# Third layer of a four-layer AdaLN/FFN kernel: conditioning by 32x32 products, a two-strip router, and the share added by accumulating transfers

## What is computed

```python
def _L2_cond_ref(x, embedding, W0, b0, W1, b1, W2, b2, weight, bias_k):
    h = jax.nn.gelu(embedding @ W0 + b0, approximate=False)
    h = jax.nn.gelu(h @ W1 + b1, approximate=False)
    att = jax.nn.softmax((h @ W2 + b2) / T, axis=-1)      # 64 x 8
    agg_w = jnp.einsum('bk,koi->boi', att, weight[..., 0]) # a 32x32 matrix for each sample
    agg_b = att @ bias_k
    return jnp.einsum('boi,bih->boh', agg_w, x) + agg_b[:, :, None]

def _L2_ffn_ref(hidden_states, router_weight, router_bias, expert_bias):
    flat = hidden_states.reshape(T, H)                     # 2048 x 512
    logits = jnp.einsum('th,eh->te', flat, router_weight) + router_bias   # 64 experts
    scores = jax.nn.softmax(logits, axis=-1)
    topk_w, topk_idx = jax.lax.top_k(scores, 8)
    w_sum = topk_w.sum(axis=-1, keepdims=True)
    w_dense = jnp.zeros((T, E)).at[jnp.arange(T)[:, None], topk_idx].add(topk_w)
    bias_mix = jnp.einsum('te,eh->th', w_dense, expert_bias)
    return flat * w_sum + bias_mix
```

## Time and profile before

| | us |
|---|---|
| median of 3 runs | 560.16 |
| lowest, highest | 559.52, 560.53 |
| the profiled execution | 559.38 |
| its span | 557.6 |

### The profile page before, as it was taken

One profiled execution on the slowest core, in us unless ns is written; L12 is line 12 of the kernel. 1 busy time (PEld: TensorE's weight loads), 2 busy tenths in 40 slices (PEclk: granted clock), 3 DMA queues, 4 the chain that ended last, 5 costly groups with the idle time before them and its releaser, 6 DMA issues.

```text
span 557.6 us, 7199 instructions
## 1 busy us (share of the span) xinstructions
PE 543.6 (97%) x2689; PEld 418.3 (75%) x2689; DVE 256.3 (46%) x529; ACT 129.9 (23%) x227; POOL 192.5 (35%) x176
## 2 busy tenths in 40 slices
PE   7999999999999999999999999999999999989996
PEld 5788888888888888888888876353535799867784
DVE  3542343622225422126223327173442388897775
ACT  4322222322223222223222221000020022244332
POOL 2699990400001200002105700300002044589996
PEclk9999999999999999999999999999999999999999
DMA  9498230293000400000313007897920333120413
GB/s 311 151 421 308 76 97 0 75 155 89 0 0 0 132 37 0 0 0 1 94 41 94 1 0 100 146 142 213 164 84 12 94 96 94 19 38 2 150 59 113
DMA packets 84212, 50.33 MB, mean 90 GB/s; under 512 B 69600, under 2 KB 74464, under 8 KB 83424
## 3 DMA queue, kind: packets, MB, share of 16 engines
q1 hardware_dynamic: 82096, 38.97, 31.8%
q0 software_dynamic: 2016, 11.01, 5.5%
q10 hardware_dynamic: 80, 0.08, 0.0%
HBM read 31.93 MB, written 8.62 MB: 73 GB/s over the span
## 4 chain that ended last, share of the span: by engine, by line
PE 92%; DVE 5%; issue 1%; ACT 1%; DMA 1%; POOL 0%; DVEq 0%; POOLq 0%
PE ps L547 91%; DVE c_lo L963 1%; DVE cT L963 1%; DMA pack_a<-in_pack_a 1%; DVE t L963 0%; DVE rest L1145 0%; PE ps L693 0%; PE ps L731 0%; PE ps L787 0%; PE ps L737 0%; DVE wcat L963 0%; DVE c_lo_odd L963 0%; DVE m L1141 0%; DVE lg L963 0%; DVE rest L963 0%
## 5 line engine op out<-in xcount | busy, mean ns | idle before, releaser
L547 PE MATMUL ps<-c_lo,wl 128*128 128x512 f32 x448 | 173.0, 390 | 0.3 <-POOL c_lo L422 0.3
L547 PE MATMUL ps<-c_hi,wl 128*128 128x512 f32 x448 | 173.1, 390 | 0.2
L963 DVE TENSOR_TENSOR hff<-silu,ps 128x512 f32<-128x512 f32 x56 | 38.5, 687 | 160.3 <-PE ps L547 160.2
L547 PEld LDWEIGHTS ps<-c_lo,wl 128*128 128x128 f32 x448 | 84.1, 188 | 18.6 <-POOL c_lo L422 0.7
L547 PEld LDWEIGHTS ps<-c_hi,wl 128*128 128x128 f32 x448 | 84.1, 188 | 18.2 <-ACT c_hi L849 0.8
L547 PE MATMUL ps<-wl,h_hi 128*128 128x512 f32 x224 | 87.7, 391 | 0.0
L547 PE MATMUL ps<-wl,h_lo 128*128 128x512 f32 x224 | 87.2, 389 | 0.0
L963 DVE TENSOR_TENSOR h_lo<-hff,h_hi 128x512 fp32r<-128x512 f32 x56 | 49.0, 875 | 39.1 <-ACT h_hi L849 39.1
L422 POOL TENSOR_TENSOR c_lo<-cT,c_hi 128x512 fp32r<-128x512 f32 x8 | 10.7, 1341 | 156.9 <-ACT c_hi L849 156.9
L849 ACT ACTIVATE h_hi<-hff 128x512 fp32r<-128x512 f32 x56 | 35.4, 632 | 112.5 <-DVE hff L963 112.5
L883 ACT ACTIVATE silu<-ps 128x512 f32<-128x512 f32 x56 | 33.5, 598 | 116.4 <-PE ps L547 116.4
(11 more groups left out here) (163 smaller groups left out, 630.4 us busy)
## 6 DMA issues: line engine op xcount, KB each, us to landing
wl<-in_wl POOLq DMA_DIRECT2D x14, 768.0 KB, 9.8
stg<-y_dram SPq DMA_DIRECT2D x64, 128.0 KB, 5.1
xs<-in_x SPq DMA_DIRECT2D x4, 1024.0 KB, 8.0
x_all<-in_x SPq DMA_DIRECT2D x1, 4096.0 KB, 14.3
y_dram<-prod SPq DMA_DIRECT2D x16, 256.0 KB, 2.2
xs<-x_all SPq DMA_DIRECT2D x4, 1024.0 KB, 5.3
out_x<-x_all SPq DMA_DIRECT2D x16, 256.0 KB, 2.0
bias_bc<-bias_dram SPq DMA_DIRECT2D x15, 256.0 KB, 5.0
```

What stands on the lines that cost most here:

```text
L547: return pe.matmul(o, l, r, start=start, stop=stop)
L963: return dve.tensor_tensor(o, a, b, op)
```

## The change

**Rows as they are, mixed by 32x32 products.** The third layer's conditioning no longer uses `blk` and `xs` turned. SyncE writes each group's x to DRAM (`spill`) and reads it back so that the 32 rows of a sample stand on one strip of 32 partitions, tile j on strip j, samples beside each other (`fetch`, into `xT(g)`: the convolution's `stg` for the groups 0 and 1, `xs` for 2, `osc` for 3). A sample's rows are then mixed by one product of its 32x32 matrix with 512 columns: strip j of the array's rows, strip b of its columns, bank j (`mix_rows`, sixteen for a group). For this the masks and attention tables of this layer are built differently at the start: five small POOL operations ahead of the first weight loads, one product more for the table, four small ones for the bias by token (`biasN`).

**Turning.** ACT takes the mixed rows out with their bias (`rows_out`, into `cS[g]`, one buffer for each group, laid over `c_hi`, `c_lo`, `c_hi_odd`, `c_lo_odd`), TensorE turns them (`turn_c`), VectorE copies them to `cT` (`store_c`).

**Router.** 64 experts on two strips of 64 output columns, 256 tokens each, 8 products (`router2`); ACT adds the bias while it copies the 128x256 logits to `lgT2`, TensorE turns them by two transposes (`turn_logits2`), VectorE copies them to `logit`.

**Route.** The choice and the weights come by four fused operations instead of a comparison and a product; the sums, the reciprocal and the share stand behind the weights.

**Experts.** Their products go to the banks 5, 6, 7, 5, so the fourth waits for the first `final2` (`experts2`).

**Share.** ACT scales `cS[g]` in place; POOL issues one transfer for a group which adds it to `x_all` in SBUF (`accum_op`), behind that group's `final2`. The fourth layer's conditioning waits for the transfer (`s_cS_added`). Rounds are written out, not looped. The fourth layer's second group uses the banks 0 to 3 and its own bias table (`bias_odd`), loaded early.

The core of the diff:

```diff
-                sp.wait_ge(s_cond_mm[before], done)
-                sp.wait_ge(s_x_new[1], (g + 1) * GT)
-                sp.dma_start(xs[:], x_all[:, g * GT:(g + 1) * GT, :]).then_inc(s_staged[2], 16)
+            def spill(g):
+
+                sp.wait_ge(s_x_new[1], GT * (g + 1))
+                dst = x_dram[g * TOK:(g + 1) * TOK].rearrange("(j p) n -> p j n", p=P)
+                sp.dma_start(dst, x_all[:, g * GT:(g + 1) * GT, :]).then_inc(s_x_dram[g], 16)
+
+            def fetch(g):
+
+                sp.wait_ge(s_x_dram[g], 16)
+                if g == 0:
+                    sp.wait_ge(s_cond_mm[1], G * Q)
+                if g == 2:
+                    sp.wait_ge(s_cond_mm[0], G * S)
+                for j in range(GT):
+                    src = x_dram[(g * GT + j) * P:(g * GT + j + 1) * P].rearrange("(b i) n -> i b n", b=TB)
+                    sp.dma_start(xT(g)[j * ROWS:(j + 1) * ROWS], src).then_inc(s_xT[g], 16)
...
-            for g in range(G):
-                stage(g)
-                bias(2, g)
-            for g in range(G):
+            spill(0)
+            spill(1)
+            fetch(0)
+            fetch(1)
+            spill(2)
+            fetch(2)
+            bias(3, 0)
+            spill(3)
+            fetch(3)
+            for g in range(1, G):
...
             def add_scaled(g):
-                pool.wait_ge(s_staged[2], (g + 1) * 16)
-                for j in range(GT):
-                    pool.wait_ge(s_t1, g * GT + j + 1)
-                    xg = x_all[:, ds(g * GT + j, 1), :]
-                    pool.tensor_tensor(xg, xg, t1[:, j:j + 1, :], ALU.add).then_inc(s_t1_added, 1)
-
...
+                pool.wait_ge(s_x_new[2], GT * (g + 1))
+                pool.wait_ge(s_cS_scaled, GT * (g + 1))
+                pool.dma_start(x_all[:, g * GT:(g + 1) * GT, :], cS[g][:], accum_op=ALU.add).then_inc(s_cS_added[g], 16)
...
                 if l == 3:
-                    pe.wait_ge(s_x_new[2], GT * (g + 1))
+                    pe.wait_ge(s_cS_added[g], 16)
...
-                    cond(2, 0, SPARING, [nothing, nothing, nothing, lambda: (turn_hm(g), pe.wait_ge(s_cT[2], 1))])
-                    lora_b(g)
-                    pe.wait_ge(s_w_lo, 3)
-                    pe.wait_ge(s_weights23, 16 * 8)
-                    router2(0)
...
+            def mix_rows(g, js):
+
+                for j in js:
+                    at = slice(j * ROWS, (j + 1) * ROWS)
+                    for b in range(TB):
+                        ins = mm(bank(base2(g) + j)[b * ROWS:(b + 1) * ROWS], agg[at, 1, g * GT + b], xT(g)[at, b])
+                    ins.then_inc(s_cond_mm[2], 1)
+
+            def turn_c(g):
+
+                for n, j in enumerate(order2(g)):
+                    pe.wait_ge(s_cS, GT * g + n + 1)
+                    for s in range(S):
+                        ins = pe.transpose(bank(base2(g) + j)[:, cols(s)], cS[g][:, j, cols(s)], ident)
+                    ins.then_inc(s_c_turned, 1)
 
             def router2(g):
-                pe.wait_ge(s_cT[2], S * (g + 1))
-                for j in range(GT):
-                    for s in range(S):
-                        ins = mm(bank(4)[:, j * P:j * P + NPAD], cT[:, s, cols(j)], wr2[:, s], s == 0, s == S - 1)
+                pe.wait_ge(s_cT[2], GT * (g + 1))
+                for s in range(S):
+                    c = cT[:, s].rearrange("p (a h n) -> p h a n", a=2, h=2)
+                    for h in range(2):
+                        ins = mm(bank(4)[h * E2:(h + 1) * E2, 0:2 * P], wr2[:, s, 0:E2], c[:, h], s == 0, s == S - 1)
                 ins.then_inc(s_router2, 1)
+
+            def turn_logits2(g):
+                pe.wait_ge(s_lgT2, g + 1)
+                for a in range(2):
+                    ins = pe.transpose(bank(4)[:, (2 + a) * P:(3 + a) * P], lgT2[:, cols(a)], ident)
+                ins.then_inc(s_logits2, 1)
...
-            def layer2(g, more):
-                for j in range(GT):
-                    for s in range(S):
-                        ins = pe.transpose(bank(j)[:, cols(s)], cT[:, s, cols(j)], ident)
-                    ins.then_inc(s_c_back, 1)
-                l, h = (2, g + 1) if more else (3, 0)
-                cond(l, h, SPARING, [nothing, nothing, nothing,
-                                      lambda: (turn_weights(g), pe.wait_ge(s_cT[l], S * h + 1))])
+            def experts2(g):
                 pe.wait_ge(s_wT2, g + 1)
                 for j in range(GT):
-                    pe.wait_ge(s_t1, GT * g + j + 1)
-                    mm(bank(j), wT[:, cols(j)], eb_hi[:], True, False)
-                    mm(bank(j), wT[:, cols(j)], eb_lo[:], False, True).then_inc(s_product[2], 1)
-                if more:
-                    router2(g + 1)
-                    pe.wait_ge(s_x_new[2], GT * (g + 1))
-                else:
-                    pe.wait_ge(s_w_hi, 4)
-                    router3(0)
+                    if j == GT - 1:
+                        pe.wait_ge(s_x_new[2], GT * g + 1)
+                    b = bank(SPARING[j])
+                    mm(b, wT[:, cols(j)], eb_hi[:], True, False)
+                    mm(b, wT[:, cols(j)], eb_lo[:], False, True).then_inc(s_product[2], 1)
+
+            def last1(g):
+                base(g)
+                pe.wait_ge(s_hm, g + 1)
+                turn_hm(g)
+                pe.wait_ge(s_xT[0], 16 * GT)
+                pe.wait_ge(s_pool_step, MIXED2)
+                mix_rows(0, (1, 2, 3))
+                lora_b(g)
+                mix_rows(0, (0,))
+                turn_c(0)
+
+            def layer2(g):
+                turn_logits2(g)
+                turn_c(g + 1)
+                turn_weights(g)
+                experts2(g)
+                router2(g + 1)
+                if g + 2 < G:
+                    pe.wait_ge(s_xT[g + 2], 16 * GT)
+                    mix_rows(g + 2, range(GT))
+
+            def last2(g):
+                turn_logits2(g)
+                cond(3, 0, range(S), [nothing] * S)
+                turn_weights(g)
+                experts2(g)
+                pe.wait_ge(s_w_hi, 4)
+                router3(0)
...
+            def rows_out(g, places):
+                for n in places:
+                    j = order2(g)[n]
+                    act.wait_ge(s_cond_mm[2], GT * g + n + 1)
+                    act.activation(cS[g][:, j], bank(base2(g) + j), ACT.Identity,
+                                   bias=biasN[:, g * GT + j:g * GT + j + 1]).then_inc(s_cS, 1)
...
+            def layer2(g):
+                act.wait_ge(s_router2, g + 1)
+                act.activation(lgT2[:], bank(4)[:, 0:2 * P], ACT.Identity, bias=rbT[:]).then_inc(s_lgT2, 1)
+                if g + 1 < G:
+                    rows_out(g + 1, range(1))
                 exp(s_shifted2, s_exp2, g, E2)
...
+                if g + 1 < G:
+                    rows_out(g + 1, range(1, GT))
                 act.wait_ge(s_wcat_turned, g + 1)
                 copy(wT[:], bank(4)).then_inc(s_wT2, 1)
...
+            def store_c(g):
+
+                for n, j in enumerate(order2(g)):
+                    dve.wait_ge(s_c_turned, GT * g + n + 1)
+                    dve.tensor_copy(cT[:, :, j * P:(j + 1) * P],
+                                    bank(base2(g) + j).rearrange("p (s n) -> p s n", s=S)).then_inc(s_cT[2], 1)
...
-            cond(2, 0, SPARING)
             dve.wait_ge(s_base_bias, NT)
-            residual(1, G - 1)
+            residual(1, G - 1, (0, 1))
+            store_c(0)
+            residual(1, G - 1, (2, 3))
...
+                link = linker(before2, PER2, g)
+                lt = bank(4)[:, 2 * P:4 * P].rearrange("p (j e) -> p j e", j=GT)
+                dve.wait_ge(s_logits2, g + 1)
+                link(dve.tensor_copy(logit[:], lt), True)
...
                 for j in range(GT):
                     ins = dve.match_replace(rest[:, j], m8[:, j], logit[:, j], LOWEST)
                 link(ins)
-                link(tt(rest[:], rest[:], logit[:], ALU.not_equal))
                 dve.wait_ge(s_exp2, g + 1)
+                for j in range(GT):
+                    ins = dve.scalar_tensor_tensor(lg[:, j], rest[:, j], LOWEST, ex[:, j], ALU.is_equal, ALU.mult)
+                link(ins)
+                link(dve.tensor_copy(wcat[:, :, 0:E2].bitcast(F32R), lg[:]))
+                tt(wcat[:, :, E2:2 * E2], lg[:], wcat[:, :, 0:E2], ALU.subtract).then_inc(s_wcat, 1)
                 dve.tensor_reduce(stat[:, 1], ex[:], AX, ALU.add)
-                link(tt(lg[:], ex[:], rest[:], ALU.mult))
-                dve.reciprocal(stat[:, 2], stat[:, 1])
-                dve.tensor_reduce(stat[:, 0], lg[:], AX, ALU.add)
-                link(dve.tensor_copy(wcat[:, :, 0:E2].bitcast(F32R), lg[:]))
+                if g:
+                    dve.wait_ge(s_cS_scaled, GT * g)
+                link(dve.tensor_reduce(stat[:, 0], lg[:], AX, ALU.add))
+                link(dve.reciprocal(stat[:, 2], stat[:, 1]))
```

(2 more changed lines are left out.)

254 lines of the change are left out of this document (162 added, 92 removed).

## The result

The changed kernel takes 573.25 us (median of 4, 572.11 to 574.02), the kernel before 560.35 beside it: ratio 1.0227, interval 1.0208 to 1.0245. Forecast were 562.1, range 558.2 to 569.5. The profiled execution shown here took 572.11, its span is 569.9.

The account below looks back on a forecast made before the run. Bound: TensorE, 97% busy, but the third layer loops between VectorE and TensorE. Entry +2.3, two rounds +0.37 each, one -0.72, exit -0.4 sum to +1.9 us: 561.3 profiled, 562.1 median; range 558.2 to 569.5.

Parts of the forecast that it names:

- the start of the sum: Ahead of the third layer: the second layer's last base products end at 435.35 in both kernels, no shift.
- Start: Kernel start: POOL's masks delay its first weight loads 1.5 to 2 us; four tiny TensorE products cost 0.1 at most.
- The clock: Third layer: forecast would be wrong if TensorE's granted clock, 1.00 so far, dropped there; no size or chance given.
- The sign: Whole kernel: slower, by a sum of +1.9 us; chance of slower 0.64, of faster 0.20.
- The mixing: Third layer: sixteen 32x32 products of 512 columns on TensorE take 1.7 us a round, range 1.0 to 3.9.
- rival A: Third layer: mixing takes 1.0 and router 1.7 us, so the kernel is faster, 558.6 us; chance 0.15.
- C: Rival, mixing: row strips do not overlap, mixing takes 3.6 us, 568.9 us in all; chance 0.20.
- D: Rival, mixing: a 32x32 product's second record blocks the next product, 6.9 a mixing, about 582 us; chance 0.06.
- B: Rival, VectorE's four copies from PSUM: twice an add's pace, 1.4 us instead of 2.5, 558.0 us; chance 0.06.
- The fourth expert pair: Third layer: last expert pair, 0.46 us, waits for the bank freed by VectorE's first final operation; next router stands behind.
- E: Rival, transfers: the accumulating one or a fetch lands late, some 3 to 5 us, about 566 us; chance 0.05.
- Up to about 1 us of slip is covered: POOL's last transfer issue before the bias additions: its 1.37 us idle ahead of the first split absorbs the delay, cost nothing.

Follow-up runs that it names:

- a4_same: Changed kernel with biasN and rbT allocated behind other tiles, so wl0 begins where it did in the kernel before; 564.64 us, ratio 1.0087.
- a5_both: a4_same plus idle TensorE products at three places where TensorE waited in the third layer; 560.39 us, ratio 1.0002.
- a2_at128: Changed kernel with rbT behind wT and an unused 64-byte tile behind biasN, putting wl0 on a multiple of 128 bytes; 572.08 us, ratio 1.0200.
- v5_pair: a5_both with the fourth expert pair behind the next router and GpSimd waiting for VectorE's two splits; 559.51 us, ratio 0.9973.
- v1_pair: a2_at128 with the fourth expert pair issued behind the next router instead of ahead of it; 579.67 us, ratio 1.0356.
- v4_loop: a4_same with v1_pair's edit, mixing behind the logits' turn, two row copies ahead of the exponents, GpSimd waiting for VectorE's splits; 557.56 us, ratio 0.9948.
- v9_after_route: v4_loop with ACT sharing turned-row copies, GpSimd's split wait dropped, four bias additions before its last transfer but after VectorE's route; 553.83 us, ratio 0.9900.

## Why the prediction was wrong, by its own steps

- **The failed step is the start of the sum.** "The products of the second layer's last group end at 435.35 in both": all that lies ahead of the third layer was put at nothing, except for *Start* (the masks and four tiny products), which was costed at nothing as well, and rightly to within a few tenths (a4_same has that place at 436.05, a5_both at 435.75, 0.7 and 0.4 later). But the diff also moves tiles. The runs showed 444.81 in place of 435.35, and 8.7 of these 9.46 us are the place of `wl0`: two thirds of the loss.
- **The clock.** "It would be wrong if TensorE's granted clock ... dropped in the emptier third layer": it did, but it had no price and no chance. It was worth 1.7 + 0.3 us in the profiled execution (13.70 and 12.31 against the 12.02 of a5_both), 3.0 in a2_at128 and 4.2 in a4_same. The other three runs of the changed kernel had a mean granted clock of 0.983 or 0.984, the profiled one 0.991. The prediction counted only whether TensorE was waited for, not how much it idled.
- **The sign was luck.** With the tiles in their old place and the clock held (a5_both) the ratio is 1.0002 (0.9990 to 1.0014): no change, where the sum had +1.9. What made the changed kernel slower was what the sum lacked.
- **The mixing was mis-sized.** 1.7 was taken, 1.07 to 1.08 measured (456.20 to 457.28, 1.07 in the next two). It was rival A's 1.0: the row strips run at once. C and D fell. The 0.8 added for the issue of 32 records, at the strip router's pace, was wrong: four products took 0.99, twelve 1.04, sixteen 1.07, so a further product added some 7 ns. The rule of the Trainium skill that the prediction cites ("TensorE: Matmul & The Clock Gate", Measured speedup vs the span model) has one product and some 4 ns for each further tile; the trace agrees with its form and has 7.
- **The other terms held.** Route 4.74 (forecast 4.7), weights ready at T + 3.75 (3.8), four copies out of PSUM 2.48 (2.5, B fell, at the pace of the adds), router 1.87 (1.9). ACT's logits copy with its signals took 0.57 (0.61). Entry, from the base products to the first logits, 12.94 (13.55), exit 8.60 (8.51). A round at full clock 12.02 (12.52; the difference is mostly the mixing), the one without mixing 11.58 (11.43).
- **The fourth expert pair** waited 0.73 in round three and 1.11 at the exit, for VectorE's first final operation, as foreseen. In rounds one and two the slow clock hid it. That VectorE's order sets the round was confirmed by v5_pair, to 0.1.
- **ACT's order was overlooked.** TensorE waited 1.63 in each round behind the first turned tile, since ACT's exponents stand ahead of its other three row copies and wait for VectorE. It cost no round its length, but it emptied TensorE, where the clock fell.
- **Transfers** were rightly costed at nothing. E fell; GpSimd's issues took 0.85 to 0.92 and not 0.59, and its pause ahead of the split shrank from 1.37 to 0.35:

```profile
505.49 0.85 POOL L603 DMA_DIRECT2D x_all<-cS  x1 [10.74 <-DVE x_all L1331]
506.06 5.28 POOL L620 TENSOR_TENSOR x_all<-x_all,bias 128x512 f32<-128x512 f32 x4
...
512.68 2.97 POOL L615 TENSOR_TENSOR c_lo<-cT,c_hi 128x512 fp32r<-128x512 f32 x2 [0.35 <-ACT c_hi L992]
```

"Up to about 1 us of slip is covered" was true with 0.35 us to spare: in v1_pair, where the last issue came 1.3 us later against the router, the cover was gone, and it wasn't 1 us that was lost but 7.

## What to carry to other kernels

When a diff allocates or drops a tile, list the places of all tiles behind it and compare, for the products that carry the time, the distance of their two operands modulo 256 bytes: here an unused tile of 32 or 128 bytes cost 9.2 or 8.6 us, more than any single edit of the third layer won. Where a change takes work from the bound engine without shortening the loop, look at that engine's granted clock in the emptied stretch; idle products there won 3.0 and 4.2 us, and v4_loop, which moves real work into one of its waits, had the clock at 1.00 through the third layer without them. And price the slip of an engine off the path by what it then runs into: read which of its instructions next stands beside a VectorE instruction with two SBUF inputs.

## What the runs showed of the hardware

- Products of 128x128 by 512 columns in fp32r came every 0.227 us with both operands at the same residue of 256 bytes, and mostly every 0.230 to 0.234 otherwise.
- Sixteen 32x32 products with 512 columns took 1.07 us, twelve of them 1.04 and four 0.99.
- In the changed kernel the granted clock fell with TensorE busy 3.4 of 5 us in the stretch before (455 to 460). In v9_after_route it stayed at 1.00, busy 16.25 of 20 us from 440 to 460 and 17.34 of the next 20, although it was busy only 3.48 of 5 from 445 to 450. No rule is drawn from that.
- A VectorE subtraction of two SBUF tiles of 128x512 took 0.68 us alone, 1.4 to 1.8 where it took turns with GpSimd, 3.0 where it was held through two GpSimd instructions and 8.9 through seven.
- An accumulating transfer of 1 MB from SBUF to SBUF landed 7.1 us after its issue.
